# A pre-LayerNorm block with a quantized gated FFN on 8 cores: the sixteen program blocks of the FFN merged into one, and the first column tile put into the common order

## What is computed

```python
x = L0_attn_u                                   # (1, 8192, 2048) f32
n = layernorm(x)
state = n @ W_b_rank @ W_b_state                # 2048 -> 64 -> 256
state = butterfly(state, A_factors)             # 8 levels of 2x2 on 256 states
x = x + state @ W_c_rank @ W_c_model + D_vec * n
n = layernorm(x)
Wg = (gate_w - 128) * gate_scale[:, None]       # 8192 x 2048, integers 0..255
Wu = (up_w   - 128) * up_scale[:, None]
Wd = (down_w - 128) * down_scale[:, None]       # 2048 x 8192
h = silu(n @ Wg.T) * (n @ Wu.T)
return x + h @ Wd.T
```

## Time and profile before

| | |
|---|---|
| time, median of 2 runs | 1660.99 us (1660.9 to 1661.09) |
| the profiled execution's own time | 1663.81 us |
| its span on the slowest core (core 6), first to last instruction | 1662.3 us |
| spans of the 8 cores | 1656.0 to 1662.3 us |
| TensorE busy, share of the span | 1419.8 us, 85% |
| VectorE busy | 637.6 us, 38% |
| ScalarE busy | 162.3 us, 10% |

### The profile page before, as it was taken

One profiled execution on the slowest core, in us unless ns is written; L12 is line 12 of the kernel. 1 busy time (PEld: TensorE's weight loads), 2 busy tenths in 40 slices (PEclk: granted clock), 3 DMA queues, 4 the chain that ended last, 5 costly groups with the idle time before them and its releaser, 6 DMA issues. The chain is left out here.

```text
span 1662.3 us, 16138 instructions; the slowest of 8 cores (1656.0 to 1662.3 us)
## 1 busy us (share of the span) xinstructions
PE 1419.8 (85%) x6386; PEld 625.3 (38%) x6386; DVE 637.6 (38%) x957; ACT 162.3 (10%) x201; POOL 151.2 (9%) x166
## 2 busy tenths in 40 slices
PE   0352363999999999999999999999999999999993
PEld 0110011444444444444444444444444444444441
DVE  0336917223532344224423442254225521542141
ACT  0221440100000001000100011001000100000000
POOL 6000000110011001100110011001100110011000
PEclk9965566999999999999999999999999999999997
DMA  9300000732073217321731264126422542245005
GB/s 255 64 1 0 0 0 20 152 77 43 14 156 77 46 26 152 76 41 36 152 77 27 51 137 91 26 51 121 93 41 51 104 99 51 51 89 114 1 0 202
DMA packets 31816, 119.14 MB, mean 72 GB/s; under 512 B 2752, under 2 KB 2848, under 8 KB 31744
## 3 DMA queue, kind: packets, MB, share of 16 engines
q0 software_dynamic: 27520, 101.35, 30.8%
q1 hardware_dynamic: 4224, 16.78, 3.1%
HBM read 59.98 MB, written 8.39 MB: 41 GB/s over the span
## 5 line engine op out<-in xcount | busy, mean ns | idle before, releaser
L524 PE MATMUL PG<-xln,wgbuf 128*128 128x512 bf16 x2016 | 457.1, 380 | 15.2 <-PEq L581 12.5
L530 PE MATMUL PU<-xln,wubuf 128*128 128x512 bf16 x2016 | 455.7, 379 | 0.0
L565 DVE SCALAR_TENSOR_TENSOR h_sb<-PU,us_sb,sg_sb 128x512 bf16<-128x512 f32 x128 | 96.0, 751 | 619.2 <-PE PU L530 608.6
L524 PEld LDWEIGHTS PG<-xln,wgbuf 128*128 128x128 bf16 x2016 | 197.0, 98 | 256.0 <-issue 20.8
L530 PEld LDWEIGHTS PU<-xln,wubuf 128*128 128x128 bf16 x2016 | 197.3, 98 | 237.9
L606 PE MATMUL PD<-h_sb,wd_grp 128*128 128x512 bf16 x1024 | 231.4, 379 | 12.1 <-PEq L470 12.1
L606 PE MATMUL PG<-h_sb,wd_grp 128*128 128x512 bf16 x1024 | 231.5, 379 | 0.0
L546 ACT ACTIVATE sg_sb<-PG,gs_sb 128x512 f32<-128x512 f32 x128 | 87.8, 687 | 730.8 <-PE PG L524 730.7
L606 PEld LDWEIGHTS PD<-h_sb,wd_grp 128*128 128x128 bf16 x1024 | 99.6, 98 | 134.7 <-issue 15.8
L606 PEld LDWEIGHTS PG<-h_sb,wd_grp 128*128 128x128 bf16 x1024 | 100.2, 98 | 120.8
L620 DVE SCALAR_TENSOR_TENSOR x_sb<-PG,ds_sb,x_sb 128x512 f32<-128x512 f32 x128 | 96.1, 751 | 117.2 <-PE PG L606 117.2
(11 more groups left out here) (125 smaller groups left out, 459.0 us busy)
## 6 DMA issues: line engine op xcount, KB each, us to landing
wgbuf<-wg_d POOLq DMA_DIRECT2D x64, 512.0 KB, 4.9
wubuf<-wu_d POOLq DMA_DIRECT2D x64, 512.0 KB, 6.9
wd_grp<-wd_d POOLq DMA_DIRECT2D x16, 2048.0 KB, 17.6
x_sb<-u_in SPq DMA_DIRECT2D x4, 2048.0 KB, 26.3
out_d<-x_sb SPq DMA_DIRECT2D x4, 2048.0 KB, 17.3
wbr_sb<-wbr_d POOLq DMA_DIRECT2D x1, 256.0 KB, 10.7
wcm_sb<-wcm_d POOLq DMA_DIRECT2D x1, 256.0 KB, 15.0
wbs_sb<-wbs_d POOLq DMA_DIRECT2D x1, 32.0 KB, 11.1
```

The lines of the kernel that those rows point to most:

```text
L524: mm = t.matmul(PG[par][:, :], wgbuf[:, (m % 4) * D + k * 128:(m % 4) * D + (k + 1) * 128], xln2[:, k * T + hh * 512:k * T + (hh + 1) * 51 ...
L530: mm = t.matmul(PU[par][:, :], wubuf[:, (m % 4) * D + k * 128:(m % 4) * D + (k + 1) * 128], xln2[:, k * T + hh * 512:k * T + (hh + 1) * 51 ...
L565: inc(v.scalar_tensor_tensor(h_sb[:, ml * T + hh * 512:ml * T + (hh + 1) * 512], PU[par][:, :], us_sb[:, m:m + 1], sg_sb[:, par * 512:(par ...
```

## The change

The two loops over `g` with two blocks each become one block, and every engine's list now holds its own loop over `g`. Waits that were taken from the counters at build time (`cnt["sTd"]`, `tVd0`, `tTd0`, `cnt["sdD"]`) are written as numbers of `g` with the same values. GpSimd's two loops over `mp` (six tiles in block 1, two in block 2) become one loop over eight. The special order of tile 0 is dropped: its 64 matmuls are issued in the common order, 16 for gate and 16 for up of half 0, then the same for half 1, and the waits for the chunks of `xln2` stand at the 16 matmuls of the first gate accumulation. Nothing else is changed: all other loops have the same bodies and the same waits.

```diff
-    for g in range(NG):
-        with nc.Block() as blk:
-            @blk.gpsimd
-            def _(gp):
+    with nc.Block() as blk:
+        @blk.gpsimd
+        def _(gp):
+            for g in range(NG):
                 wt(gp, "sPd", g + 1)
...
-                for mp in range(8 * g + 4, min(8 * g + 10, MC)):
+                for mp in range(8 * g + 4, min(8 * g + 12, MC)):
...
-            @blk.tensor
-            def _(t):
+        @blk.tensor
+        def _(t):
+            PDX = (PD0, PD1, PG0, PG1)
+            for g in range(NG):
                 if g > 0:
                     wt(t, "sVd", 32 * g)
-                if g == 0:
-                    wt(t, "sdG0", 16)
-                    wt(t, "sdW0", 16)
-                    for k in range(KC):
-                        wt(t, "sV", ln2_nrm + k + 1)
...
                 for ml in range(GS):
                     m = g * GS + ml
-                    if g == 0 and ml == 0:
-                        continue
                     for hh in range(2):
...
+                        first = (g == 0 and ml == 0 and hh == 0)
                         for k in range(KC):
+                            if first:
+                                wt(t, "sV", ln2_nrm + k + 1)
                             mm = t.matmul(PG[par][:, :],
...
+                wt(t, "sdD", 32 * (g + 1))
+                wt(t, "sVh", 16 * (g + 1))
+                for c in range(KC):
+                    for hh in range(2):
+                        sl = 2 * c + hh
+                        if sl >= 4:
+                            wt(t, "sVd", 32 * g + sl - 3)
+                        for ml in range(GS):
+                            mm = t.matmul(PDX[sl % 4][:, :],
...
+                        inc(mm, "sTd")
...
-            @blk.vector
-            def _(v):
+        @blk.vector
+        def _(v):
+            PDX = (PD0, PD1, PG0, PG1)
+            for g in range(NG):
                 if g > 0:
-                    wt(v, "sTd", cnt["sTd"])
+                    wt(v, "sTd", 32 * g)
                 for j in range(2 * GS):
...
-        with nc.Block() as blk:
-            tTd0, tVd0 = cnt["sTd"], cnt["sVd"]
-
-            @blk.gpsimd
-            def _(gp):
-                for mp in range(8 * g + 10, min(8 * g + 12, MC)):
...
-            @blk.tensor
-            def _(t):
-                wt(t, "sdD", cnt["sdD"])
-                wt(t, "sVh", 16 * (g + 1))
...
-            @blk.vector
-            def _(v):
-                PDX = (PD0, PD1, PG0, PG1)
                 for c in range(KC):
                     for hh in range(2):
                         sl = 2 * c + hh
-                        wt(v, "sTd", tTd0 + sl + 1)
+                        wt(v, "sTd", 32 * g + sl + 1)
```

More of the change, by code:

```diff
@@ L534, in _ @@
                         inc(mm, "sTu")
[L536 to L539, removed]
+                wt(t, "sdD", 32 * (g + 1))
[7 more added lines that the diff above has]
+                            mm = t.matmul(PDX[sl % 4][:, :],
+                                          wd_grp[:, ml * D + c * 128:ml * D + (c + 1) * 128],
+                                          h_sb[:, ml * T + hh * 512:ml * T + (hh + 1) * 512],
+                                          start=(ml == 0), stop=(ml == GS - 1))
+                        inc(mm, "sTd")
+        @blk.scalar
+        def _(s):
+            wt(s, "sdA", 144)
+            for g in range(NG):
                 for ml in range(GS):
@@ L634, in _ @@
                     inc(v.drain(), "sVd")
-        if g == 0:
-            dump("h0", h_sb[:, :], [128, GS * T], BF16)
-            dump("x0", x_sb[:, :], [128, KC * T], F32)
     ctxB.close()
```

## The result

The changed kernel takes 1650.2 us (median), where the kernel before takes 1660.99 us in the runs beside it. The ratio is 0.9935, with a 95% interval of 0.9924 to 0.9946, so it is 9.0 to 12.6 us faster: a gain clear of the scatter, and within 2% of no change. The forecast was 1650.5 us.

A forecast was written before the change was run, and what follows sets the result against it. The prediction took TensorE to bound the FFN, with 27.2 us idle. Passages 3.8 + 2.5, tile 0 2.8 and the clock 1.4 made 10.5 us, so 1660.99 - 10.5 = 1650.5 us, range 1646.5 to 1657.

The forecast's parts named there:

- What bounds the kernel: FFN: TensorE bounds it, so a change gains only from its idle time (27.2 of 1662.3 us) or low clock.
- Part 1: Passages from gate and up to down, 8 times: TensorE starts 0.14 us after VectorE instead of 0.61, saving 3.8 us.
- Part 2: Passages from down to next group, 7 times: 0.58 us after the addition instead of 0.89, plus 0.3 us; 2.5 us saved.
- Part 3: Tile 0 in common order: tile 1 no longer waits for silu table, silus and product; 2.78 us saved.
- part 4: Start of tile 1: no clock fall after the bubble, saving 1.4 us on core 6, nothing on core 7.
- The sum: Whole kernel: 3.8 + 2.5 + 2.8 + 1.4 = 10.5 us saved on core 6, 9.1 on core 7; median 1650.5 us.
- Only tile 0 gains: Rival: passages keep their length, branches run hidden under TensorE's waits on VectorE; 4.2 us saved, 1656.8 us; chance 0.16.
- waits for free: Rival at the passages: satisfied waits behind a released one cost nothing; 13.5 us saved, 1647.5 us; chance 0.10.
- Slower by fetching: Rival: TensorE's run of over 12,000 instructions waits for some 54 fetched packets, up to 65 us, 1715 us; chance 0.02.
- The branch: The 15 passages: by the skill's rule each would hold a 1.2 us fetch, 18 us; the prediction used measured 0.61 and 0.89 us.

The follow-up runs named there:

- e5_half_waits: Changed kernel with finer waits: after each passage the first accumulation waits for 15 of 16 products or 31 of 32 additions, the second for all; 1628.72 us.
- e3_release_last: Changed kernel with the wait for the last addition put behind the four long satisfied waits at the 7 starts of a new group; 1647.74 us.
- e4_waits_added: Changed kernel with four more long satisfied waits behind the released one at each of the 15 passages; 1659.79 us.
- e1_merged_only: Changed kernel with tile 0 put back into its own order, so that only the branches and barriers go; 1655.32 us.
- e8_all: Changed kernel with finer waits, FFN joined to the second LayerNorm, tile 0 in old order, group 0's wd_grp fill and load behind tile 1; 1618.97 us.

## Why the prediction was right, point by point

- **What bounds the kernel.** TensorE's idle time in the FFN is what the change had to work on. Removing all that was left of it at the passages, 18.8 us as shown and 21.3 counted from start to start, brought the time down by 20.7 us in e5_half_waits.
- **Part 1, 8 passages to the down products, 3.8 us.** Measured 12.1 - 8.6 = 3.5 us: the prediction took the first passage, 1.54 us, for all eight, and most take 1.50. The release takes 0.15 us (forecast 0.14), the idle 1.07 us (forecast 1.0 to 1.1).
- **Part 2, 7 passages to a new group, 2.5 us.** Measured 12.5 - 10.2 = 2.3 us; 0.57 us behind the addition (forecast 0.58). That four satisfied waits make up most of this 0.57 was argued in the prediction and is shown by e3_release_last and e4_waits_added. The seven average 1.46 us where the first has 1.43, so a small spread stays without the branches, and the 0.3 us counted for it came back only in part.
- **Part 3, tile 0, 2.8 us, and part 4, the clock behind it, 1.4 us on core 6.** Alone they gave 4.4 us where the sum is 4.2. The fall costs 1.4 us on core 6, but 1.6 to 1.7 on the other four cores that it hit. Which cores are hit is not fixed (0, 1, 2, 4 and 6 before, 0, 3, 4 and 7 in e1_merged_only), but in each of these two executions some were, and they set the time.
- **The sum.** 10.5 us forecast, 10.8 measured. The prediction took core 6 and core 7 as the slowest for good. They were so in that execution for a reason outside the FFN: its first matmul came at 274.86 and 275.20 us on them and at 269.9 to 271.9 us on the others. So the sum of spans came out near for a core that is not the slowest as a rule (in the profiled execution of the changed kernel it is core 4), and that is luck; the difference of the medians does not rest on it. That 10.5 and 10.8 lie so close is luck too, with an interval of 9.0 to 12.6 us; the parts, measured one by one, are what bears the prediction out.
- **The rivals.** "Only tile 0 gains" is refuted by e1_merged_only, "waits for free" by e3_release_last. "Slower by fetching": in the run of over 12,000 instructions TensorE shows no idle but at the 15 passages, and the changed kernel is not slower.
- **The branch.** The prediction set the rule of the Trainium skill (Runtime: NRT & Kernel Launch, "Instruction fetch mechanics") against the trace. The passages gave back 0.44 and 0.33 us each on average, barrier included, and not the 1.2 us of a fetched packet: the trace did not bear out a full stall at these branches. The rule speaks of targets outside the fetched pages; whether these targets were, no view shows. Nor do the runs tell the branches' share from the barrier's, since every kernel here has both or neither.

## What to carry to other kernels

When a barrier is taken out of a passage, subtract first what the data itself makes one wait for: here 18.8 of the 24.6 us of idle time stayed without the barriers, most of it VectorE's last instruction and its hand-over. A finer wait, which lets TensorE begin with the half that is ready, removed all of it and brought 20.7 us, three and a half times the 5.8 us of the 15 barriers. Put the wait that is really waited for last, because each satisfied one behind it costs 0.11 us. And an order written for an overlap is worth nothing while a barrier lies in between, and little when the engine that must release the next step has other work queued first: look at that engine's queue before joining two stages.

## What the runs showed of the hardware that was not expected

- The fall of TensorE's clock from 2.4 to 1.2 GHz after a short idle is not a matter of its length alone. After 2.62 or 2.63 us it fell on five of eight cores in the kernel before, on four in e1_merged_only and on all eight in e8_all; after 2.00 us in 7 of 15 passages of e4_waits_added, and on one core both ways. After the 1.94 us and less of the other passages it fell in none. It costs 1.3 to 1.7 us each time, and the slowest core decides, so lengthening 15 stops by 0.4 to 0.5 us each cost 9.5 us in place of 7.0.
- The idle time that the profile shows ahead of a matmul is 0.16 us short of the hole in the sequence, since matmuls are shown 0.38 us long and follow one another every 0.216 us. Over 15 stops this makes 2.5 of the 21.3 us by which e5_half_waits shortened the FFN stretch.
